# GRU recurrence started after a short early convolution, with the rest of the convolution placed between its products

## The chip, the cores and the metric

The kernel runs on one core of a Trainium2 chip. The metric is the device time of one execution in microseconds (us); lower is better.

## The reference

`x` is (128, 64, 512): batch B, steps T, channels D. `cond` (128, 512) serves twice: as the taps of a depthwise causal convolution and as the GRU's first state.

```python
y = conv_general_dilated(x, cond[:, None, :], window_strides=(1,), padding=[(127, 0)],
                         feature_group_count=512, ...) + b     # causal, one kernel per channel
x = x + y
# GRU over 64 steps, h0 = cond, on rows x[:, t]
gi = x_t @ W_ih + b_ih;  gh = h @ W_hh + b_hh                  # (128, 1536) each
r = sigmoid(i_r + h_r);  z = sigmoid(i_z + h_z);  n = tanh(i_n + r * h_n)
h = (1 - z) * n + z * h
out = x + swapaxes(hs, 0, 1)
```

The sequence axis of `x` has 64 steps, of the 128 taps the last 64 count. Of a channel, y is a 64 x 64 triangular Toeplitz matrix times the channel's (64, 128) slab of x. `x` in float32 is 16.8 MB, `W_ih` and `W_hh` 3.1 MB each. The kernel runs the recurrence over the steps of x in reverse row order of its scratch (`T - 1 - t`), because the Toeplitz matrices are built reversed.

## The kernel before, in words

**Stage one, convolution.** SP loads all of x into SBUF (`x_sb`, L328): channels in two halves c, each with steps on 64 partitions for two groups of 128 channels (`half`). Meanwhile TensorE builds the Toeplitz matrices by shifting the taps (L678), ACT and DVE copy them out (`toep_span`). Then 512 matmuls of 128x128 in full float32 (L695, `bank<-diag,x_sb`) convolve a pair of channels each; ACT spreads the Toeplitz matrices into block-diagonal `diag` (L496), DVE evicts each bank with the bias into `stage` or `kept` (L578), and SP stores these to the scratch tensor `xres` in HBM (L317, L335). The weights come behind them on SP's queue (L362), 32 partitions per DMA.

**Weights.** fp32r products carry a float32 number as two parts: ACT copies the high part (L513), DVE and POOL subtract for the low part (L297).

**Stage two, recurrence.** 64 steps, each 72 matmuls of 128x512 in fp32r (L715: for each of six gate products, four blocks of 128 channels by three products of parts): h into r, n, z; then, for the next step, x into r and n; four transposes of h (L704); x into z. The order is written out in `step`, the same on each engine: L525 for ACT, L610 for DVE, L764 for PE, L416 for SP. Between them DVE adds biases (L623, L629, L631, L640), ACT does sigmoid and tanh (L532, L534, L536), and DVE forms h and out (L642 to L655). SP stores `out_t` and loads x of four steps later, once with 256-byte runs (`xt`, L372) and once transposed by quads with 128-byte runs (`x_quads`, L380).

## Time and profile before

| what | value |
|---|---|
| device time, three runs | 1250.76, 1250.97, 1252.44 us; median 1250.97 |
| span of the profiled execution | 1249.1 us |
| PE busy | 1207.4 us (97%), x5508 |
| DVE busy, ACT busy, POOL busy | 663.6, 343.1, 16.0 us |
| DMA queue q1 (SP's) | 246848 packets, 91.45 MB, 31.9% of 16 engines |
| bytes over the span | 74 GB/s mean |

The page gives no device time of the profiled execution itself; its span lies 1.9 us under the median of the runs. PE is TensorE's matmuls, PEld its weight loads, DVE is VectorE, ACT ScalarE, POOL GpSimd, SP SyncE, which issues most DMAs. A matmul's busy time is longer than its spacing, as matmuls overlap in the pipeline: the distance between starts is what one costs in a full stream. A DMA share over 1 means that packets' recorded times overlap.

### The profile page before, as it was taken

The page shows a single profiled execution, that of the slowest core. Times are in us where ns is not written, and L with a number is a line of the kernel's source. Part 1 is how long each engine was busy: PE and PEld are TensorE (multiplying, and loading weights), DVE is VectorE, ACT ScalarE, POOL GpSimd, SP SyncE. Part 2 cuts the span into 40 slices and gives each one's busy share as a digit, 9 for nine tenths or more (in the row PEclk, how much of TensorE's full clock was granted, in tenths as well). Part 3 has the DMA queues.
Part 4 walks back from the last instruction along what each step waited for, and adds up shares of the span by engine and source line. Part 5 has one row for each costly group of instructions (what it writes and reads, how often), then busy time and mean ns, then how long its engine had stood idle before and what let it go on. Part 6 is the DMA issues. An engine that isn't in the chain of part 4 may idle for free.

```text
span 1249.1 us, 14699 instructions
## 1 busy us (share of the span) xinstructions
PE 1207.4 (97%) x5508; PEld 1019.2 (82%) x5508; DVE 663.6 (53%) x1015; ACT 343.1 (27%) x474; POOL 16.0 (1%) x20
## 2 busy tenths in 40 slices
PE   5499989999999999999999999999999999999998
PEld 5499978888888888888888888888888888888886
DVE  5255685555555455555555555555555555555554
ACT  6266661212212122212221211222121212122111
POOL 1000040000000000000000000000000000000000
PEclk9699999999999999999999999999999999999999
DMA  9996758222112222221222222122222211222200
GB/s 189 208 265 214 160 159 270 51 51 51 46 38 42 50 50 50 50 46 38 42 50 50 50 50 47 38 41 50 50 50 50 47 39 40 50 50 50 50 18 18
DMA packets 247730, 92.55 MB, mean 74 GB/s; under 512 B 203168, under 2 KB 236704, under 8 KB 246432
## 3 DMA queue, kind: packets, MB, share of 16 engines
q1 hardware_dynamic: 246848, 91.45, 31.9%
q10 hardware_dynamic: 864, 0.85, 0.3%
q8 instruction: 12, 0.20, 0.1%
q14 instruction: 6, 0.05, 0.0%
HBM read 58.72 MB, written 33.55 MB: 74 GB/s over the span
## 4 chain that ended last, share of the span: by engine, by line
PE 94%; DMA 4%; ACT 1%; POOL 0%; DVE 0%; SPq 0%; issue 0%; ACTq 0%; DVEq 0%
PE bank L715 83%; PE bank L695 9%; DMA x_sb<-in_x_dram 4%; PE bank L704 2%; ACT w_ih_hi L513 1%; ACT w_hh_hi L513 0%; POOL w_hh_lo L297 0%; DVE stage L578 0%; SPq L328 0%; DVE h_less_n L646 0%; DVE h L648 0%; DVE pre_z L640 0%; ACTq L317 0%; SPq L312 0%; ACT xT_hi L505 0%
## 5 line engine op out<-in xcount | busy, mean ns | idle before, releaser
L715 PE MATMUL bank<-w_ih_hi,xT_hi 128*128 128x512 f32 x768 | 305.5, 398 | 1.3 <-DVE w_ih_lo L297 1.1
L715 PE MATMUL bank<-w_hh_hi,hT_hi 128*128 128x512 f32 x768 | 298.9, 389 | 1.2 <-DVE w_hh_lo L297 0.8
L715 PE MATMUL bank<-w_ih_hi,xT_lo 128*128 128x512 f32 x768 | 300.0, 391 | 0.0
L715 PE MATMUL bank<-w_ih_lo,xT_hi 128*128 128x512 f32 x768 | 299.3, 390 | 0.0
L715 PE MATMUL bank<-w_hh_hi,hT_lo 128*128 128x512 f32 x768 | 298.8, 389 | 0.0
L715 PE MATMUL bank<-w_hh_lo,hT_hi 128*128 128x512 f32 x768 | 298.8, 389 | 0.0
L715 PEld LDWEIGHTS bank<-w_hh_hi,hT_hi 128*128 128x128 f32 x768 | 144.2, 188 | 31.8 <-issue 1.9
L715 PEld LDWEIGHTS bank<-w_ih_hi,xT_hi 128*128 128x128 f32 x768 | 144.3, 188 | 30.9 <-POOL w_ih_lo L297 1.0
L715 PEld LDWEIGHTS bank<-w_ih_hi,xT_lo 128*128 128x128 f32 x768 | 144.1, 188 | 31.0
L715 PEld LDWEIGHTS bank<-w_hh_hi,hT_lo 128*128 128x128 f32 x768 | 144.2, 188 | 29.9
L715 PEld LDWEIGHTS bank<-w_hh_lo,hT_hi 128*128 128x128 f32 x768 | 144.2, 188 | 29.9
L715 PEld LDWEIGHTS bank<-w_ih_lo,xT_hi 128*128 128x128 f32 x768 | 144.5, 188 | 28.2
L695 PE MATMUL bank<-diag,x_sb 128*128 128x128 f32 x512 | 112.9, 385 | 26.2 <-DMA x_sb<-in_x_dram 24.9
L564 DVE TENSOR_TENSOR hT_lo<-bank,hT_hi 128x512 fp32r<-128x512 f32 x64 | 44.3, 692 | 174.5 <-ACT hT_hi L539 174.5
L695 PEld LDWEIGHTS bank<-diag,x_sb 128*128 128x128 f32 x512 | 112.5, 313 | 26.6 <-issue 26.6
L539 ACT ACTIVATE hT_hi<-bank 128x512 fp32r<-128x512 f32 x63 | 37.7, 598 | 283.3 <-PE bank L704 283.3
L631 DVE TENSOR_TENSOR new_h<-bank,bias_hh 128x512 f32<-128x512 f32 x64 | 44.2, 691 | 127.8 <-PE bank L715 127.8
L534 ACT ACTIVATE n_gate<-pre_n 128x512 f32<-128x512 f32 x64 | 40.4, 632 | 224.6 <-DVE pre_n L636 224.6
L496 ACT ACTIVATE diag<-toep_span 64x512 f32<-64x512 f32 x64 | 74.7, 1168 | 59.5 <-PE bank L695 58.7
L629 DVE TENSOR_TENSOR pre_r<-bank,bias_rz 128x512 f32<-128x512 f32 x64 | 44.2, 691 | 78.9 <-PE bank L715 78.9
L532 ACT ACTIVATE r<-pre_r 128x512 f32<-128x512 f32 x64 | 40.4, 632 | 155.3 <-DVE pre_r L629 155.3
L623 DVE TENSOR_TENSOR new_x<-bank,bias_ih 128x512 f32<-128x512 f32 x64 | 44.3, 692 | 54.2 <-PE bank L715 52.5
(54 smaller groups left out, 796.6 us busy)
## 6 DMA issues: line engine op xcount, KB each, us to landing
xt<-xres SPq DMA_DIRECT2D x128, 128.0 KB, 2.6
out_dram<-out_t SPq DMA_DIRECT2D x64, 256.0 KB, 2.1
x_quads<-xres SPq DMA_DIRECT2D x252, 64.0 KB, 2.4
x_sb<-in_x_dram SPq DMA_DIRECT2D x2, 4096.0 KB, 35.3
...
```

The source lines that it names most:

```text
L496: m = nc.scalar.activation(diag[p % 2][rows, :].rearrange("s (i h u) -> s i h u", i=PIECE, h=2)[:, :, half, :], toep[c][rows, i0 * T:(i0 + ...
L513: nc.scalar.activation(hi[which][:, cols], raw[which][:, cols], ACT.Copy).then_inc(w_hi_ready, 1)
L532: nc.scalar.activation(r[:, :], pre_r[:, :], ACT.Sigmoid).then_inc(r_ready, 1)
L534: nc.scalar.activation(n_gate[:, :], pre_n[:, :], ACT.Tanh).then_inc(n_ready, 1)
L539: nc.scalar.activation(hT_hi[:, :], ps_hT[:, :], ACT.Copy).then_inc(hT_hi_ready, 1)
L564: nc.vector.tensor_tensor(lo_out[:, :], full[:, :], hi_in[:, :].bitcast(F32), ALU.subtract).then_inc(lo_ready, 1)
L623: nc.vector.tensor_tensor(new_x[:, :], ps_in[:, :], bias_ih[:, N:NG], ALU.add).then_inc(new_x_ready, 1)
L629: nc.vector.tensor_tensor(pre_r[:, :], ps_r[:, :], bias_rz[:, R:R + D], ALU.add).then_inc(pre_r_ready, 1)
L631: nc.vector.tensor_tensor(new_h[:, :], ps_hn[:, :], bias_hh[:, N:NG], ALU.add).then_inc(new_h_ready, 1)
L695: mm = nc.tensor.matmul(bank[m % 8][:, j % BPAIRS * P:(j % BPAIRS + 1) * P], x_sb[c][:, :].rearrange("s (b i) -> s i b", b=B)[:, i0 + j, : ...
L704: mm = nc.tensor.transpose(psum[:, k * P:(k + 1) * P], block_of(k), ident[:, 0:P])
L715: mm = nc.tensor.matmul(psum[:, :], a[:, rows], w[which][:, cols], start=start and n == 0, stop=stop and n == 2)
```

## The change

The convolution is split in time. Names new in it:

- **Early part.** The steps 0 to 15 (`EARLY`) of all channels are convolved first, in float32: `x_early` holds 8 groups of 64 channels on 16 partitions each (eight DMAs, 4.2 MB, 256-byte runs), `toep_early` is laid out from `kernel_full` in HBM by 16 DMAs on ACT's queue (64-byte runs). 64 matmuls of 128x128 (L698), DVE evicts them into `early_result`, 16 banks, two ahead of each block of weights it splits (L590). SP stores the result in four quarters of eight DMAs (L292), each from 16 partitions (4.2 MB in all), behind all weight loads.
- **Step 0** takes its x row from `x_row` directly. On ACT it waits for x of step 1 (`xT_loaded`), whose load SP issues after all quarters are stored, and for `early_stored`, before its first sigmoid.
- **Bulk part.** The 48 other steps of all channels (as a 64 x 64 product) are convolved in 128 banks of two pairs of channels: four matmuls of 128x256 in fp32r each (L730). Up to ten banks go between the 24 blocks of products of each of the steps 1 to 13 (`bulk_bank`, `POINTS`). x comes a second time, in 8 units of 64 channels with 128-byte runs into 64 partitions (2.1 MB each, two buffers); the Toeplitz matrices come from `kernel_parts` in HBM by overlapping rows (64 blocks, 262 KB each, 256-byte runs, four buffers). ACT copies the high part of x (`split`), DVE subtracts the low part; a bank is evicted half by ACT (`first_half`, two operations of 128 columns), half by DVE (`second_half`). The result is stored in 16 stages of two DMAs from 48 partitions (786 KB the two).
- **Recurrence.** Same 72 matmuls and four transposes per step. Biases are written into PSUM by ACT ahead of the products (`put_bias`, four per step), so that DVE's four bias additions go; `x_quads` and its transpose go; x is loaded transposed, 512-byte runs (`load_xT`); out is formed transposed and turned by DVE (L657, L664), stored by four DMAs.

```diff
-SLICE = 32
-PIECE = 8
+EARLY = 16
+POINTS = 10
+BULK_FIRST, BULK_LAST = 1, 13
...
-            load_x(0, 0, B)
-            load_x(1, 0, 3 * QUARTER)
+            for c in range(C0):
+                sp.dma_start(
+                    x_early[c * EARLY:(c + 1) * EARLY, :].rearrange("s (b g) -> s b g", g=G0),
+                    x[:, 0:EARLY, c * G0:(c + 1) * G0].rearrange("b s g -> s b g"),
+                ).then_inc(x_early_loaded, 16)
+            for n in range(QUARTERS):
+                sp.wait_ge(early_evicted, (n + 1) * NB0 // QUARTERS)
+                per = G0 // QUARTERS
+                for c in range(C0):
+                    e = place_of(c * G0 + n * per)
+                    sp.dma_start(xres[LATE:T, e:e + per, :].rearrange("u g b -> u (g b)"),
+                                 quarter[n][c * EARLY:(c + 1) * EARLY, :]).then_inc(early_stored[n], 16)
...
+            def load_xT(u, back):
+                sp.dma_start(
+                    xT[u][:, :].rearrange("p (k b) -> p k b", b=B),
+                    xres[bass.ds(back, 1), :, :].rearrange("o (k p) b -> p (o k) b", p=P),
+                ).then_inc(xT_loaded[u], 16)
...
+                    ch = unit * 2 * UNIT + c * UNIT
+                    bs = slice(b4 * B // 4, (b4 + 1) * B // 4)
+                    sp.dma_start(
+                        x_unit[unit % 2][c * T:(c + 1) * T, :].rearrange("s (b g) -> s b g", g=UNIT)[:, bs],
+                        x[bs, :, ch:ch + UNIT].rearrange("b s g -> s b g"),
+                    ).then_inc(x_unit_loaded[unit % 2], 16)
...
+                    source = bass.AP(first.tensor, first.offset, [[1, T], [P, 2 * BLOCK], [1, T]])
+                    sp.dma_start(
+                        toep[j % T_RING][c * T:(c + 1) * T].bitcast(F32).rearrange(
+                            "s (n e) -> s n e", e=P)[:, :, c * T:(c + 1) * T],
+                        source,
+                    ).then_inc(toep_loaded[j % T_RING], 16)
...
+                    e = place_of(unit * 2 * UNIT + c * UNIT + g)
+                    sp.dma_start(xres[0:LATE, e:e + STAGE, :].rearrange("u g b -> u (g b)"),
+                                 stage[n % 2][c * T:c * T + LATE, :]).then_inc(stage_stored[n % 2], 16)
...
+            for n in range(QUARTERS):
+                sp.wait_ge(early_stored[n], 16 * C0)
+            load_xT(1, T - 2)
+            sp.wait_ge(early_done, NB0)
+            sp.wait_ge(k_parts_stored, 16 * QUADS)
+            for b4 in range(4):
+                load_x_quarter(0, b4)
+            for j in range(T_RING):
+                load_toep(j)
+            load_xT(2, T - 3)
+            load_xT(3, T - 4)
+            for b4 in range(4):
...
+                if m % 2 == 0 and m >= 2 and m // 2 + 3 < NBLOCK:
+                    sp.wait_ge(conv_done, m)
+                    load_toep(m // 2 + 3)
+                if m % 8 == 2 and m > 2:
+                    store_stage(m // 8 - 1)
+                unit, b4 = (m + 21) // 16, (m + 21) % 16 // 2
+                if m % 2 and 2 <= unit < NUNIT and b4 < 4:
+                    if b4 == 0:
+                        sp.wait_ge(x_lo_ready, (unit - 1) * UNIT // BLOCK)
+                    load_x_quarter(unit, b4)
...
-                    rows = slice(half * T, (half + 1) * T)
-                    m = nc.scalar.activation(
-                        diag[p % 2][rows, :].rearrange("s (i h u) -> s i h u", i=PIECE, h=2)[:, :, half, :],
-                        toep[c][rows, i0 * T:(i0 + PIECE) * T].rearrange("s (u i) -> s i u", u=T), ACT.Copy)
+                for c in range(C0):
+                    first = kernel_full[c * G0 + half * G0 // 2:(c + 1) * G0, T - EARLY:T]
+                    act.dma_start(
+                        toep_early[half][c * EARLY:(c + 1) * EARLY, :].rearrange(
+                            "s (g e) -> s g e", e=P)[:, :, c * EARLY:(c + 1) * EARLY],
+                        bass.AP(first.tensor, first.offset, [[1, EARLY], [P, G0 // 2], [1, EARLY]]),
+                    ).then_inc(toep_early_loaded[half], 16)
...
+            def put_bias(psum, bias, done):
+                nc.scalar.activation(psum[:, :], bias, ACT.Copy).then_inc(done, 1)
...
+                if j >= HL_RING:
+                    act.wait_ge(conv_done, 2 * (j - HL_RING) + 2)
+                unit = j // (UNIT // BLOCK)
+                act.wait_ge(x_unit_loaded[unit % 2], 16 * 8 * (unit // 2 + 1))
+                nc.scalar.activation(part_block(j, 0), x_block(j), ACT.Copy).then_inc(x_hi_ready, 1)
...
+                    nc.scalar.activation(tmp[m % 2][:, pair * B:(pair + 1) * B],
+                                         conv_bank[m % 3][:, pair * 2 * B:pair * 2 * B + B], ACT.Identity,
+                                         bias=bias_pair[:, 2 * m + pair:2 * m + pair + 1]).then_inc(tmp_ready, 1)
...
+                first_half(bulk_bank(t - 1, POINTS - 1))
+                if not last(i, u):
+                    act.wait_ge(xT_loaded[(u + 1) % RING], 16 * (i + 1))
+                    act.wait_ge(gi_done, t + 1)
+                    nc.scalar.activation(xT_hi[:, :], xT[(u + 1) % RING][:, :], ACT.Copy).then_inc(xT_hi_ready, 1)
+                split(split_block(t, 0))
+                first_half(bulk_bank(t, 0))
+                if not isinstance(i, bass.RuntimeValue) and t == 0:
+                    for n in range(QUARTERS):
+                        act.wait_ge(early_stored[n], 16 * C0)
+                act.wait_ge(gh_r_done, t + 1)
+                nc.scalar.activation(r[:, :], ps_r[:, :], ACT.Sigmoid).then_inc(r_ready, 1)
...
+                if not isinstance(i, bass.RuntimeValue) and t == BULK_FIRST - 1:
+                    split(0)
+                    split(1)
...
-                nc.vector.tensor_tensor(
-                    stage(g).rearrange("b (u h i) -> b i h u", h=2, i=SLICE)[:, i0:i0 + BPAIRS],
+                if g == R:
+                    for _ in range(2):
+                        early_evict(evicted)
+                        evicted += 1
+                if not on_pool(w, k, g):
+                    dve.wait_ge(w_hi_ready, n + 1)
+                    low_weights(nc.vector, w, k, g).then_inc(w_lo_ready, 1)
...
+                nc.vector.tensor_tensor(
+                    stage[s % 2][:, at:at + 2 * B].rearrange("p (g b) -> p g b", b=B),
+                    conv_bank[m % 3][:, :].rearrange("p (g l b) -> p g l b", l=2, b=B)[:, :, 1, :],
+                    tmp[m % 2][:, :].rearrange("p (g b) -> p g b", b=B),
+                    ALU.add).then_inc(stage_ready, 1)
...
-                for j in range(PIECE):
-                    m = (p * PIECE + j) // BPAIRS
-                    mm = nc.tensor.matmul(
-                        bank[m % 8][:, j % BPAIRS * P:(j % BPAIRS + 1) * P],
-                        x_sb[c][:, :].rearrange("s (b i) -> s i b", b=B)[:, i0 + j, :],
-                        diag[p % 2][:, j * P:(j + 1) * P], start=True, stop=True)
+                if slot == 0 and n >= 3:
+                    pe.wait_ge(early_evicted, n - 2)
+                mm = nc.tensor.matmul(conv_bank[n % 3][:, slot:slot + B], toep_early[half][:, g_half * P:(g_half + 1) * P],
+                                      x_early[:, :].rearrange("p (b g) -> p g b", g=G0)[:, g, :],
+                                      start=True, stop=True)
...
+                if m >= 3:
+                    pe.wait_ge(stage_ready, m - 2)
+                elif m == 0:
+                    pe.wait_ge(early_evicted, NB0)
+                if m % 2 == 0:
+                    j = m // 2
+                    pe.wait_ge(toep_loaded[j % T_RING], 32 * (j // T_RING + 1))
+                    pe.wait_ge(x_lo_ready, j + 1)
+                for pair in range(2):
+                    j, slot = (2 * m + pair) // BLOCK, (2 * m + pair) % BLOCK
+                    for low in range(2):
+                        at = (slot * 2 + low) * P
+                        mm = nc.tensor.matmul(conv_bank[m % 3][:, pair * 2 * B:(pair + 1) * 2 * B],
+                                              toep[j % T_RING][:, at:at + P],
+                                              parts[j % HL_RING][:, slot * 2 * B:(slot + 1) * 2 * B],
+                                              start=low == 0, stop=low == 1)
+                mm.then_inc(conv_done, 1)
...
+                        g = group[0]
+                        group[0] += 1
+                        if g * POINTS // GROUPS != (g + 1) * POINTS // GROUPS:
+                            bulk(bulk_bank(t, g * POINTS // GROUPS))
...
+                pe.wait_ge(hT_lo_ready, t + 1)
+                product(ps_r, hT_hi, hT_lo, 1, R, True, gh_r_done)
+                pe.wait_ge(bias_hn_put, t + 1)
+                product(ps_hn, hT_hi, hT_lo, 1, N, True, gh_n_done)
+                product(ps_z, hT_hi, hT_lo, 1, Z, True, gh_z_done)
```

SP's queue at the start. Before, from the first DMA to the weights:

```order
L312 DMA taps_sb<-in_cond_dram 64x2x128
L328 DMA x_sb_49<-in_x_dram 64x128x128 x2
L328 DMA x_sb_50<-in_x_dram 64x96x128 x2
L317 DMA xres<-stage_60 128x2048 [waits stage_ready]
...
L335 DMA xres<-stage_64 128x4096 [waits stage_ready]
L362 DMA w_ih_raw<-in_L_cond_W_ih_dram 32x1536 [waits xres_stored2,diag_ready]
```

The same place in the change, up to the loads of the bulk part:

```order
L271 DMA h<-in_cond_dram 128x4x32 x4
L271 DMA x_row<-in_x_dram 128x4x32 x4
L277 DMA x_early<-in_x_dram 16x128x64 x8
L285 DMA w_ih_raw<-in_L_cond_W_ih_dram 32x1536 x16
L285 DMA w_hh_raw<-in_L_cond_W_hh_dram 32x1536 x16
L292 DMA xres<-early_result_93 16x2048 [waits early_evicted]
...
L296 DMA xT_75<-xres 128x4x128 [waits early_stored2,early_stored3,early_stored1,early_stored0]
L305 DMA x_unit_55<-in_x_dram 64x32x32 [waits k_parts_stored,early_done]
L305 DMA x_unit_55<-in_x_dram 64x32x32 x7
L316 DMA toep_ring<-kernel_parts 64x8x64 x8
```

The weights moved ahead of every store; the stores, 128 partitions wide before, are 16 wide, and x of step 1 is loaded only behind them.

ACT in step 0 of the change (`r` is the first gate):

```order
L513 ACTIVATE xT_hi_79<-xT1_75 128x512 [waits gi_done,xT_loaded1]
L520 ACT_TABLE_LOAD [waits early_stored3,early_stored2,gh_r_done,early_stored1]
L520 ACTIVATE r_66<-bank0 128x512 [waits early_stored0]
L469 ACTIVATE bank0<-bias_rz_81 128x512 [waits r_ready]
L528 ACTIVATE n_gate_68<-q_69 128x512 [waits pre_n_ready]
```

Before, ACT had no wait for a store there; now the first sigmoid stands behind the load of x of step 1 and behind all quarters.

PE in step 1 of the change, from its first product of h:

```order
L708 MATMUL bank<-w_hh_hi,hT_hi 128x512 [waits hT_lo_ready]
L708 MATMUL bank<-w_hh_lo,hT_hi 128x512
L708 MATMUL bank<-w_hh_hi,hT_lo 128x512
...
L730 MATMUL bank<-x_parts_58,toep_ring 128x256 [waits x_lo_ready,toep_loaded0,early_evicted]
L730 MATMUL bank<-x_parts_58,toep_ring 128x256 x3
L708 MATMUL bank<-w_hh_hi,hT_hi 128x512
```

A bank of the convolution (four matmuls) stands after the third block of products, and so on at ten places of the step; the products behind it on PE wait with it.

## Rows read from the trace of the kernel before

**Rows 1.** The page: span, and the chain that ended last, by engine

```profile
span 1249.1 us, 14699 instructions
...
PE 94%; DMA 4%; ACT 1%; POOL 0%; DVE 0%; SPq 0%; issue 0%; ACTq 0%; DVEq 0%
```

**Rows 2.** The chain in order of time: start us, us, what (x count)

```profile
2.42 44.97 DMA x_sb<-in_x_dram
47.64 56.41 PE bank L695 x256
...
105.34 56.46 PE bank L695 x256
...
189.74 0.44 PE bank L704 x4
190.18 16.37 PE bank L715 x72
206.99 16.38 PE bank L715 x72
...
1232.00 10.93 PE bank L715 x48
1242.95 0.70 DVE pre_z L640
```

**Rows 3.** Timeline of PE near 10 us, 256-column fp32r matmuls: start us, us, instruction

```profile
10.11 0.28 PE L678 MATMUL bank<-taps_lo,window 128*128 128x256 f32 x1
10.22 0.28 PE L678 MATMUL bank<-taps_hi,window 128*128 128x256 f32 x1
```

**Rows 4.** Windows: stretch, us, busy of PE PEld DVE ACT POOL, PEclk, DMA share, GB/s

```profile
9.00:20.00 11.00, 11.00 (x94) 11.00 (x94) 10.78 (x24) 10.72 (x23) 0.00 (x0) 1.00 1.23 205
78.00:82.00 4.00, 4.00 (x20) 4.00 (x19) 2.56 (x3) 2.67 (x3) 0.00 (x0) 1.00 1.01 426
122.00:132.00 10.00, 10.00 (x48) 10.00 (x47) 5.72 (x7) 6.50 (x7) 0.00 (x0) 1.00 1.02 219
132.00:136.00 4.00, 4.00 (x20) 4.00 (x19) 2.58 (x3) 2.83 (x3) 0.00 (x0) 1.00 1.11 244
175.00:177.00 2.00, 1.74 (x8) 1.48 (x9) 2.00 (x5) 1.60 (x4) 0.84 (x1) 1.00 1.05 292
259.00:260.00 1.00, 1.00 (x7) 0.81 (x5) 0.38 (x1) 0.00 (x0) 0.00 (x0) 1.00 0.99 157
```

**Rows 5.** DMA issues: queue op xcount, KB each, us to landing

```profile
out_dram<-out_t SPq DMA_DIRECT2D x64, 256.0 KB, 2.1
xt<-xres SPq DMA_DIRECT2D x128, 128.0 KB, 2.6
```

**Rows 6.** Timeline of SP near 257 us: start us, us, instruction xcount

```profile
257.31 2.05 SPq L380 DMA_DIRECT2D x_quads<-xres  x4
```

**Rows 7.** Windows, TensorE idle and started again: columns as in Rows 4

```profile
26.00:28.00 2.00, 0.00 (x0) 0.00 (x0) 0.00 (x0) 1.86 (x2) 0.00 (x0) 0.55 1.24 215
51.00:53.00 2.00, 2.00 (x12) 2.00 (x10) 1.05 (x1) 1.51 (x2) 0.00 (x0) 0.50 1.22 205
53.00:55.00 2.00, 2.00 (x11) 2.00 (x11) 1.15 (x2) 0.95 (x2) 0.00 (x0) 0.88 1.22 205
```

**Rows 8.** Groups by line and shape: busy us, mean ns, idle before

```profile
L496 ACT ACTIVATE diag<-toep_span 64x512 f32<-64x512 f32 x64 | 74.7, 1168 | 59.5 <-PE bank L695 58.7 <-DVE toep_span L558 0.4
L646 DVE TENSOR_TENSOR h_less_n<-z,h_less_n 128x512 f32<-128x512 f32 x64 | 44.4, 693 | 10.7 <-ACT z L536 10.6
L532 ACT ACTIVATE r<-pre_r 128x512 f32<-128x512 f32 x64 | 40.4, 632 | 155.3 <-DVE pre_r L629 155.3
L539 ACT ACTIVATE hT_hi<-bank 128x512 fp32r<-128x512 f32 x63 | 37.7, 598 | 283.3 <-PE bank L704 283.3
L578 DVE TENSOR_TENSOR stage<-bank,conv_bias 128x512 f32<-128x512 f32 x32 | 32.1, 1033 | 55.9 <-PE bank L695 55.9
L530 ACT ACT_TABLE_LOAD x15 | 19.2, 1283 | 22.9 <-DVE xT L618 22.9
L505 ACT ACTIVATE xT_hi<-bank 128x256 fp32r<-128x256 f32 x2 | 0.7, 373 | 4.9 <-PE bank L737 4.9
```

924 lines of the change are left out of this document (431 added, 493 removed).

## Prediction

> **What bounds the kernel now.** I read the page first: the chain that ended last is TensorE for 94% and DMA for 4% of the 1249.1 us span [rows 1]. The chain in order of time then splits the span in two [rows 2]. Until 162 us it is the convolution: 45.0 us of waiting for the first half of x, then twice 56.4 us of matmuls. From 189.74 us on it is the recurrence: 72 matmuls in 16.37 us (0.2273 us each) and four transposes in 0.44 us, 16.80 us a step, to the last products at 1242.93 us; 6.2 us of gates and store follow. The reader should see that a step has no idle time on PE, and that before the first full step 190 us pass. The change can only win in those 190 us, and it pays for it inside the steps. From the windows I then read what DMAs reach by shape, since the change replaces wide transfers by narrow ones.
>
> **What goes.** Waiting for half of x, both convolution stretches and the wait for the last weights, all before 189.74 us. DVE's bias additions and the transpose of x lie beside a busy PE: nothing gained.
>
> **Rates of the DMAs.** Into 64 partitions x comes at 205 GB/s; from 128 partitions the stores leave at 426, or 3.3 GB/s for each partition; into 32 partitions at a time the weights come at 219 to 244, say 230, or 7.2 per partition; bias rows into 128 partitions (with others) at 292; 128-byte runs into 32 partitions at 157 [rows 4]. So 64 partitions get half of what 128 get, and 32 as much as 64. For 16 partitions the trace has no row. Upper end: 230, if again nothing is lost. Lower end: 51, the 3.2 per partition of the 64. I take 16 x 7 = 110, since 7 per partition is about the highest that any row shows, and the 32-partition row is the nearest. The Trainium skill ("SBUF — State Buffer", Door 1: The DMA port swizzle) says that bandwidth goes by how many of 16 ports the partitions reach, eight for both 32 and 64, and lists 104 GB/s for partitions 0 to 15; this trace agrees for 64 against 128 and has nothing on 16. By that page's 104 the two terms of 38 us below would be 40 us each. For 256-byte runs into 64 partitions the ends are 157 and 205; I take 180, the middle.
>
> **The start, to the moment E at which the early result is stored.** SP's queue is served in order.
> - Eight loads of h and x_row, each issued in 0.51 us (2.05 for four [rows 6]), from 0.8 us: 4.9 us.
> - x_early, 4.19 MB at 110 GB/s: 38 us, to 43.
> - ACT's queue shares the engines: 8192 runs of 64 bytes at no more than the 0.82 ns that a 128-byte run takes (128 B at 157 GB/s): 6.7 us, and 2.3 MB of other data at 292: 7.9. I take 12 of these 14.6, as a little falls before x_early starts (ends 0 and 14.6). To 55.
> - Weights, 6.29 MB at 230: 27.3 us. To 82.3.
> - The quarters, 4.19 MB at 110: 38.1, and 2.1 to land [rows 5]. E = 122.5.
>
> Beside this: 64 early matmuls at 0.22 us, or 0.44 at half clock (256 in 56.41 at mostly full clock, rows 2), are 14 to 28 us from 55 on; weights are split as they come; the products of step 0 end by about 100. That is hidden under the stores; without that cover it would be the bound at 95 to 100.
>
> **Step 0 after E.** Load of x for step 1: 0.5 + 2.6 [rows 5]; high part 0.63, table load 1.28, r 0.63, bias into PSUM 0.6 [rows 8]: E + 6.3. Then 24 products 5.5, transposes 0.4, 12 products 2.7. PE has stood still for over 20 us; in the trace it fell to half clock (0.55, then 0.50) when idle and needed about 6 us of matmuls to come back [rows 7], here 3 us of loss. Step 0 ends at E + 18.
>
> **Steps 1 to 15.** 15 x 16.80 = 252.0. The bulk adds 512 matmuls of 256 columns; such a stream has starts 0.117 us apart [rows 3]: 59.7. Together 312.
>
> Do the other engines keep up? A full bulk step lasts 16.80 + 40 x 0.117 = 21.5 us. ACT: nine operations of 512 at 0.6, twenty of 128 columns at 0.26 (from 0.598 for 512 and 0.373 for 256 [rows 8]), five splits that read with a stride; L496, with a stride, takes 1.17, against 0.63 without. Sum 5.5 + 5.2 + 5.9 = 16.6. DVE: nine at 0.69, ten at 0.42, five at 1.03 (as L578): 15.6. Both fit. The tightest place is hT_hi, which stands behind three splits and four evictions: about 7.7 us of ACT from gh_z on, against 7.3 of PE, then 1.4 to the low part of h, covered by 12 products and two banks (3.7 us). About 1.5 us is left.
>
> DMA hardly fits. Per 16 banks, 34.3 us of PE: one unit of x 2.1 MB at 157, 13.4; eight Toeplitz blocks 2.1 MB at 180, 11.7; two stages 1.57 MB from 48 partitions, at 205 as for 64: 7.7 (ends 3.7 at 426 and 14 at 110); out and transposed x of 1.6 steps, 3.7. That is 36.4, 2 over, eight times: 17 us, less what the prefetch of four blocks absorbs. I take 10 (ends 0 and 50). Bulk also starts with a backlog: unit 0, four blocks and x of two steps stand in the queue before unit 1, so that x of step 2 arrives at about E + 24, and ACT's r of step 1 behind it: 5 us. Named after the wait: PE at the bulk matmul stands for `toep_loaded` or `stage_ready`, and the products of the gates wait behind it. Step 15 ends at E + 18 + 312 + 15 = E + 345.
>
> A second rule of the skill ("DMA: Bandwidth & Descriptors", How a descriptor splits into AXI transactions) charges a run that starts off a 256-byte boundary for bytes that it fetches and drops. The Toeplitz rows start 4 bytes apart, so nearly all are such runs. No row of this trace has one. By that page a run would take 15 instead of 11 beats on average, and a block a third longer, which would be worth an estimated 25 us more; it is in neither sum.
>
> **Steps 16 to 63.** 47 x 16.80 = 789.8, 36 products 8.2. Then z 0.63, two DVE operations 1.4, transposes 0.6, two DVE operations 1.4, four DMA issues 1.5, landing 2.1: 7.6, against 6.2 now.
>
> **Sum.** 122.5 + 345 + 789.8 + 8.2 + 7.6 = 1273 of span, against 1249.1. The median of the runs lies 1.9 us over the profiled span: 1275 us, slower by 24 us (1.9%). Before gave 189.74 us to the start; now step 0's transposes come at E + 15, or 137; 52 us are won there, and 60 of bulk matmuls, 15 of waits and 1.4 at the end are paid.
>
> **Rivals.**
> - *Faster: 16 partitions cost nothing more than 32.* x_early at 230 takes 18, the quarters 18 at 230, or 10 at 426: 40 to 48 us less, 1227 to 1235; with stage stores at 426 too the waits of 10 go: 1217. Price 1225. The decision falls at about 160 GB/s for both. For it: 32 partitions get what 64 get. Against it: 64 do not get what 128 get, so something other than the 16 engines counts. Chance 0.25.
> - *Far slower: narrow runs cost by their number.* x_sb's 512-byte runs took 2.5 ns each at 205 GB/s (512/205). If a 128-byte run of x cost half of that, 1.25 ns instead of 0.82, the bulk's 131,072 runs would take 164 us instead of 107, and DMA would bound the bulk: about 45 us more, 1320. For it: these runs come from the same tensor x as those slow ones; the row at 157 GB/s reads `xres`. Against: that row. Chance 0.10.
> - *ACT or DVE bounds the bulk.* If a split costs 1.8 us on ACT (its stride is 128 bytes, L496 read 32), ACT's 19.8 of 21.5 with waits in between puts hT_hi late by about 1 us in 13 steps: 1288. Chance 0.05, inside the range.
> - *The bulk does not fall between the products.* PE executes in order and the listed order has it there; no chance.
>
> **Numbers.** The forecast case has 0.60 and reaches by itself from 1244 (no DMA waits, ACT's queue hidden, consecutive narrow DMAs overlapping a little) to 1310 (stages at 110 GB/s). The faster rival lies at 1214 to 1243. The range of 1214 to 1310 leaves out the far slower rival and little more of the tails. About 0.2% is what a measurement here can tell from no change, 1248.5 to 1253.5: the forecast's low end puts 0.05 there, and 0.01 under it. Faster 0.26, same 0.05, slower 0.69.
>
> **What would show it.** Right: DMA at about 110 GB/s while `x_early` loads and while `early_result` is stored; the first sigmoid of step 0 at about 127 us, preceded by an idle PE at half clock; steps 14 and later at 16.80 us; steps 1 to 13 at 21.5 to 24 us with waits at L730 for `toep_ring`. Wrong: over 200 GB/s in the two narrow stretches and E near 80; or bulk steps at exactly 21.5 us, which would say that DMA fits with ease; or bulk steps over 26 us; or waits at L730 for ACT's and DVE's evictions.

## The result and the profile after

The changed kernel takes 1268.35 us (median of 4 runs, 1265.81 to 1273.29) beside 1251.57 (4 runs, 1250.76 to 1252.44): a ratio of 1.0138, 95% interval 1.0114 to 1.0162, slower by 1.4%. The forecast was 1275 and slower. The ratios here and below are those of all runs of a kernel to runs of the kernel before, taken beside them. The profiled span is 1265.0 us, forecast at 1273.

The page of the changed kernel, to be held against [rows 1]: the span, and the chain that ended last, by engine and by line.

```profile
span 1265.0 us, 14934 instructions
...
PE 86%; DMA 3%; ACTq 3%; DVE 2%; ACT 2%; SPq 2%; issue 1%; POOL 0%; DVEq 0%
PE bank L708 78%; PE bank L730 4%; DMA bias_hn<-in_L_cond_b_hh_dram 2%; PE bank L675 2%; ACTq L442 2%; SPq L305 1%; DVE w_ih_lo L255 1%; PE bank L698 1%; ACT tmp L503 1%; DMA kernel_full<-k_full 1%; ACT x_parts L493 1%; ACT bank L469 1%; SPq L316 0%; DVE early_result L581 0%; DMA xT<-xres 0%
```

The second entry of the lower row, after the products and the bulk, is a transfer that the prediction never costed: the load of `bias_hn`, 256 KB. The chain in order of time (start us, us, what) shows its place at the start, as [rows 2] did for the kernel before.

```profile
48.11 28.93 DMA bias_hn<-in_L_cond_b_hh_dram
77.04 0.07 issue
77.11 2.35 POOL bias_rz L402
79.46 0.02 issue
79.48 2.15 ACT bank L469 x4
81.64 0.56 ACT w_ih_hi L484
...
82.22 1.29 DVE w_ih_lo L255 x2
83.51 1.20 DVE early_result L581 x2
...
96.88 9.13 PE bank L698 x40
106.02 0.02 issue
106.04 0.70 DVE early_result L581
...
110.67 2.84 DMA xres<-early_result
```

Read it downwards: the last bias lands at 77.04, GpSimd adds two of them, ScalarE copies four into the banks, and only then splits the first weights (L484), 24 splits in a row. VectorE takes the low parts and, between them, the evictions of the early convolution, which free the banks for the early matmuls. The last eviction starts at 106.04, the last store lands at 113.5. The prediction had E, the same moment, at 122.5, by another road.

Windows of the changed kernel (columns as in Rows 4): x_early loading, the weights, and two moments while the quarters are stored (the first of them one microsecond long).

```profile
20.00:30.00 10.00, 0.00 (x0) 0.00 (x0) 0.00 (x0) 0.00 (x0) 0.00 (x0) 0.50 1.44 109
...
50.00:60.00 10.00, 7.54 (x34) 7.33 (x35) 2.67 (x4) 1.31 (x3) 0.00 (x0) 0.68 1.09 249
...
96.00:97.00 1.00, 0.14 (x2) 0.12 (x1) 1.00 (x3) 0.00 (x0) 0.00 (x0) 0.50 0.79 262
109.00:111.00 2.00, 2.00 (x10) 1.65 (x10) 0.00 (x0) 0.00 (x0) 0.00 (x0) 1.00 0.91 221
```

The load into 16 partitions ran at 109 GB/s; 110 was taken. The stores from 16 partitions ran at 221 to 262 in these two windows, though 110 was taken for them too.

The steps are read from the starts of hT_hi on ScalarE (timeline: start us, us, instruction, idle before and its releaser): here the end of step 0, step 1, and step 11, the longest.

```profile
128.27 0.60 ACT L547 ACTIVATE hT_hi<-bank 128x512 fp32r<-128x512 f32 x1 [4.14 <-PE bank L675]
152.76 0.64 ACT L547 ACTIVATE hT_hi<-bank 128x512 fp32r<-128x512 f32 x1
...
354.11 0.60 ACT L547 ACTIVATE hT_hi<-bank 128x512 fp32r<-128x512 f32 x1
380.43 0.60 ACT L547 ACTIVATE hT_hi<-bank 128x512 fp32r<-128x512 f32 x1
```

Steps 1 to 13 take 24.49, 22.99, 23.64, 21.77, 21.77, 23.18, 21.75, 21.91, 21.95, 22.39, 26.32, 21.78 and 20.74 us, together 294.7; from step 14 on a step is 16.80, as before. A step with ten banks and no wait is 21.77, so a bank costs 0.497 us. 13 x 16.80 + 128 x 0.497 is 282.0, and 12.7 us are waits. What a wait costs is seen in step 11 (windows, columns as in Rows 4):

```profile
365.00:370.00 5.00, 5.00 (x30) 4.33 (x29) 3.17 (x6) 3.85 (x8) 0.00 (x0) 1.00 0.81 206
370.00:375.00 5.00, 1.98 (x9) 1.45 (x8) 3.04 (x5) 2.52 (x6) 0.00 (x0) 0.88 0.74 179
375.00:380.00 5.00, 5.00 (x24) 4.28 (x23) 0.42 (x1) 1.72 (x4) 0.00 (x0) 0.78 0.94 242
```

PE stands still for 3 us in the second window, and its granted clock is 0.88 there and 0.78 in the next, where it is busy throughout and issues 24 matmuls instead of 30. A wait of 3.0 us so lengthened the step by 4.55.

What it waited for is seen on SyncE's queue (timeline of SyncE, then of PE):

```profile
363.61 1.84 SPq L327 DMA_DIRECT2D xres<-stage  x2
365.51 4.38 SPq L361 DMA_DIRECT2D out_dram<-outZ  x4
...
370.42 5.33 SPq L316 DMA_DIRECT2D toep_ring<-kernel_parts  x8
...
374.31 1.19 PE L730 MATMUL bank<-x_parts,toep_ring 128*128 128x256 f32 x4 [3.02 <-issue]
```

The next Toeplitz block is issued at 370.42, behind the store of the step's output, and landed at 374.22, 0.09 us before the matmul that needs it. The stops of PE of over 1 us at L730 in steps 2, 3 and 6 end in the same way, each 0.09 us after its block has landed. In step 1 it is another load: ScalarE stood 4.8 us for x of step 2 (`xT`), and the gates with it.

### The profile page after: what moved, and what is told of

Same layout as the page of the kernel before. It is cut to its first block, busy times and chain, and to the rows that moved or that the text cites. A ratio compares the mean times of both kernels' runs of the same rounds, so it can differ in the third digit from the quotient of the medians.

```text
span 1265.0 us, 14934 instructions
## 1 busy us (share of the span) xinstructions
PE 1180.7 (93%) x5520; PEld 982.5 (78%) x5520; DVE 536.7 (42%) x803; ACT 491.9 (39%) x928; POOL 18.9 (1%) x18
## 4 chain that ended last, share of the span: by engine, by line
PE 86%; DMA 3%; ACTq 3%; DVE 2%; ACT 2%; SPq 2%; issue 1%; POOL 0%; DVEq 0%
PE bank L708 78%; PE bank L730 4%; DMA bias_hn<-in_L_cond_b_hh_dram 2%; PE bank L675 2%; ACTq L442 2%; SPq L305 1%; DVE w_ih_lo L255 1%; PE bank L698 1%; ACT tmp L503 1%; DMA kernel_full<-k_full 1%; ACT x_parts L493 1%; ACT bank L469 1%; SPq L316 0%; DVE early_result L581 0%; DMA xT<-xres 0%
## 5 line engine op out<-in xcount | busy, mean ns | idle before, releaser
L708 PEld LDWEIGHTS bank<-w_ih_lo,xT_hi 128*128 128x128 f32 x768 | 144.9, 189 | 26.5
L631 DVE TENSOR_TENSOR q<-bank,r 128x512 f32<-128x512 f32 x64 | 44.1, 689 | 205.4 <-PE bank L708 205.4
L528 ACT ACTIVATE n_gate<-q 128x512 f32<-128x512 f32 x64 | 40.5, 633 | 173.8 <-DVE q L633 173.8
L730 PEld LDWEIGHTS bank<-x_parts,toep_ring 128*128 128x128 f32 x512 | 77.8, 190 | 22.6 <-DVE stage L613 8.0
L503 ACT ACTIVATE tmp<-bank,bias_pair 128x128 f32<-128x128 f32 x256 | 78.3, 365 | 41.0 <-PE bank L730 41.0
L513 ACT ACTIVATE xT_hi<-xT 128x512 fp32r<-128x512 f32 x63 | 39.8, 632 | 135.1 <-PE bank L708 108.3
L730 PE MATMUL bank<-x_parts,toep_ring 128*128 128x256 f32 x512 | 82.7, 284 | 8.8 <-DVE stage L613 5.5
L469 ACT ACTIVATE bank<-bias_rz 128x512 f32<-128x512 f32 x128 | 77.1, 603 | 32.2 <-POOL bias_rz L402 28.1
L602 DVE TENSOR_TENSOR x_parts<-x_unit,x_parts 128x512 fp32r<-128x512 f32 x64 | 70.6, 1104 | 38.1 <-ACT x_parts L493 38.0
## 6 DMA issues: line engine op xcount, KB each, us to landing
w_ih_raw<-in_L_cond_W_ih_dram SPq DMA_DIRECT2D x16, 192.0 KB, 13.5
```

Of the source, the lines that this page charges most:

```text
L469: nc.scalar.activation(psum[:, :], bias, ACT.Copy).then_inc(done, 1)
L503: nc.scalar.activation(tmp[m % 2][:, pair * B:(pair + 1) * B], conv_bank[m % 3][:, pair * 2 * B:pair * 2 * B + B], ACT.Identity, bias=bias ...
L513: nc.scalar.activation(xT_hi[:, :], xT[(u + 1) % RING][:, :], ACT.Copy).then_inc(xT_hi_ready, 1)
L528: nc.scalar.activation(n_gate[:, :], q[:, :], ACT.Tanh).then_inc(n_ready, 1)
L602: nc.vector.tensor_tensor(part_block(j, 1), x_block(j), part_block(j, 0).bitcast(F32), ALU.subtract).then_inc(x_lo_ready, 1)
L631: nc.vector.tensor_tensor(q[:, :], ps_hn[:, :], r[:, :], ALU.mult).then_inc(reset_h_ready, 1)
```

## Experiments

In the diffs a line of "..." marks what is left out. Steps are timed by hT_hi, as above. xT(n) is x of step n, transposed.

### The biases first

The four loads of the GRU's biases go from the end of ScalarE's queue to its head.

```diff
+            act.dma_start(bias_rz[:, :], b_ih[0:N].partition_broadcast(P)).then_inc(bias_loaded, 16)
+            act.dma_start(bias_tmp[:, :], b_hh[0:N].partition_broadcast(P)).then_inc(bias_loaded, 16)
+            act.dma_start(bias_in[:, :], b_ih[N:NG].partition_broadcast(P)).then_inc(bias_loaded, 16)
+            act.dma_start(bias_hn[:, :], b_hh[N:NG].partition_broadcast(P)).then_inc(bias_loaded, 16)
             def tap_columns(tile):
...
-            act.dma_start(bias_rz[:, :], b_ih[0:N].partition_broadcast(P)).then_inc(bias_loaded, 16)
...
```

> The four loads of the GRU's biases (1.5 MB) are issued first on ACT's queue instead of last; nothing else changes. Theory A (the start is gated by these biases: the last landed at 77.1 us, POOL's sum and ACT's four bias writes stood behind it and the split of the weights, and with it DVE's evictions of the early result, stood behind ACT): the split of w_ih begins when its first block has landed, 55 to 60 us instead of 81.6, DVE's last eviction comes at about 85 to 95 instead of 106, and the transposes of step 0 at 112 to 118 instead of 127.8; total 1250 to 1256 us. Rival B (the start is bound by the bytes of the DMA queues whatever their order, x_early, weights and stores in series): the early result is stored at most 4 us earlier and the total is 1262 us or more.

Measured: 1255.74 us (1253.31 to 1258.91, 5 runs), ratio to before 1.0038 (1.0025 to 1.0052). The chain of this kernel in order of time:

```profile
54.82 28.43 PE bank L698 x128
83.27 0.70 DVE early_result L581
...
91.00 2.90 DMA xres<-early_result
```

All 64 early matmuls (two records to each, 0.444 us together) now run in one piece. The last eviction is 22.8 us earlier, and step 0 ends at 106.49 instead of 128.27. That is 21.8 us won, but the span fell by 13.5 only: steps 1 to 13 took 303.0 instead of 294.7, with 27.0, 25.5, 25.7 and 26.9 in steps 1, 2, 6 and 11. The total lies in the range of theory A, but step 0 ended earlier than it said (112 to 118).

### The same transfers, ScalarE's order changed

The wait for the biases and the four copies of them stand behind the splits of w_ih instead of ahead of them.

```diff
-            act.wait_ge(bias_rz_ready, 1)
-            act.wait_ge(banks_opened, 1)
-            put_bias(ps_r, bias_rz[:, R:R + D], bias_r_put)
...
                 if (w, k, g) == (1, 0, R):
                     act.wait_ge(k_parts_stored, 16 * QUADS)
+                    act.wait_ge(bias_rz_ready, 1)
+                    act.wait_ge(banks_opened, 1)
+                    put_bias(ps_r, bias_rz[:, R:R + D], bias_r_put)
...
```

> The changed kernel with its transfers as they are: only ScalarE's order is changed. The wait for the four GRU biases and the four copies of them into the banks stand behind the twelve splits of w_ih and ahead of those of w_hh, not ahead of all 24. Theory A, the start is held by the splits that stand behind that wait on ScalarE's in-order queue (the biases land at 77.0, the splits start at 81.6 though w_ih is there from about 58): the w_ih splits start near 58, half of the 16 evictions follow them, and those behind w_hh's splits end near 95 instead of 106; transposes of step 0 at 117, total 1258 to 1263 with some us given back in steps 1 and 2. Theory B, what helped when the biases were loaded first was another thing (their transfers out of the way of the weights): 1267 to 1270.

Measured: 1257.17 us (1256.15 to 1259.08, 5 runs), ratio 1.0045 (1.0032 to 1.0058); just under the 1258 that was expected at best. ScalarE's timeline in this kernel:

```profile
54.11 1.67 ACT L483 ACTIVATE w_ih_hi<-w_ih_raw 128x512 fp32r<-128x512 f32 x3 [2.81 <-DMA w_ih_raw<-in_L_cond_W_ih_dram]
...
69.85 1.67 ACT L483 ACTIVATE w_ih_hi<-w_ih_raw 128x512 fp32r<-128x512 f32 x3 [3.49 <-DMA w_ih_raw<-in_L_cond_W_ih_dram]
79.32 1.12 ACT L469 ACTIVATE bank<-bias_rz 128x512 f32<-128x512 f32 x2 [7.80 <-issue]
```

The biases are put into the banks at 79.32, as late as before, and the w_ih splits go ahead of them, each triple as its weights land. Step 0 ends at 115.84, 12.4 us earlier. So 12.4 of the 21.8 us that the biases first won at the start come from the order on ScalarE alone, with every transfer where it was: the work queued behind the wait for the biases cost them. The other 9.4 are not parted here. The w_hh splits still stood behind the biases, to 81.4, and the transfers themselves are moved only in the run with the biases first.

### What the bulk costs, and what its transfers cost

First the late convolution is left out altogether.

```diff
-            if isinstance(t, int) and BULK_FIRST <= t <= BULK_LAST:
-                m = (t - BULK_FIRST) * POINTS + point
-                return m if m < NBANK else None
             return None
...
-                            load_xT(late % RING, T - 1 - late)
+                            load_xT(late % RING, LATE)
```

> The late convolution is left out altogether: its x, its Toeplitz loads, its matmuls, evictions and stores; the steps from 16 on take one row of the early result. Theory: steps 1 to 13 take 16.8 us as the others, so the difference to the change is the full price of the bulk, 59.7 to 63 us of matmuls and 15 of waits: total 1190 to 1194 us. If the bulk cost less than 70 us, the waits are not its own and lie in the start; then the total is over 1198.

Measured: 1190.2 us (1188.39 to 1190.73, 4 runs), 78 under the changed kernel; all steps from 1 on are 16.80, but step 1 with 17.26. Step 0 ends at 127.27, so the start owes the bulk 1 us at most.

In the next kernel each Toeplitz load from the fifth block on brings an eighth of its bytes.

```diff
-                    source = bass.AP(first.tensor, first.offset, [[1, T], [P, 2 * BLOCK], [1, T]])
+                    width = 2 * BLOCK if j < T_RING else 1
+                    source = bass.AP(first.tensor, first.offset, [[1, T], [P, width], [1, T]])
...
-                            "s (n e) -> s n e", e=P)[:, :, c * T:(c + 1) * T],
+                            "s (n e) -> s n e", e=P)[:, 0:width, c * T:(c + 1) * T],
```

> From the fifth Toeplitz block on each block's DMA brings one of its eight parts (an eighth of the bytes), so the late convolution is computed with other matrices; matmuls, waits and the order stay. Theory A (DMA just fails to keep up in steps 1 to 13, as in the sum's term of 10 us): steps 3, 6 and 11, which took 23.6, 23.2 and 26.3 us, come to 21.8, and the whole is 8 to 14 us faster, 1255 to 1260. Rival B (the waits in these steps come from the order of ACT and DVE, whose evictions stand behind the gates): no step changes by more than 0.3 us and the total stays within 2 us of 1268.

Measured: 1259.8 us (1257.41 to 1260.07, 4 runs), 8.5 less. By the profile the span is 7.1 us shorter. Of the 8.8 us of waits in steps 3 to 13, 7.3 are gone, and the 1.5 left lie in step 11. Step 0 ended 2.9 us earlier, which the edit doesn't explain, but steps 1 and 2 took 3.0 longer (25.9 and 24.7 us): step 2 ends at 175.9 here and at 175.8 in the changed kernel. What the span lost it lost in steps 3 to 13, where the thinned loads are.

The same was then done to the biases-first kernel, and to its x units as well:

```diff
-                    bs = slice(b4 * B // 4, (b4 + 1) * B // 4)
+                    bs = slice(b4 * B // 4, b4 * B // 4 + (B // 4 if unit < 2 else B // 32))
```

> The kernel with the biases first (1255.7 us), whose Toeplitz blocks from the fifth on and whose x units from the third on bring one eighth of their bytes, so the late convolution uses old data and its output is not the reference's; every matmul, eviction, store and issue is still there. Its steps 1 to 13 took 303.0 us against 283.0 for 13 times 16.80 and 128 banks. Theory A, transfers set what is above 283: steps 3 to 13 take 21.77 us each, what is left is at most the start's 9 us in steps 1 and 2, total 1237 to 1245, under the kernel before. Theory B, the waits are of ScalarE and VectorE (splits, tmp, stage beside the gates): they stay, 1250 or more.

Measured: 1239.27 us (1238.73 to 1240.58, 4 runs), ratio 0.9901 (0.9887 to 0.9916). Step 1 is 27.11 and every step from 2 to 12 is 21.73 to 21.78. Windows of this kernel, then of the changed kernel:

```profile
150.00:250.00 100.00, 100.00 (x536) 86.01 (x535) 70.11 (x112) 74.02 (x158) 0.00 (x0) 1.00 0.36 85
250.00:400.00 150.00, 150.00 (x796) 128.83 (x796) 100.31 (x161) 105.45 (x228) 0.00 (x0) 1.00 0.33 79
```

```profile
150.00:250.00 100.00, 96.93 (x517) 82.89 (x518) 68.55 (x110) 72.03 (x154) 0.00 (x0) 1.00 0.86 181
250.00:400.00 150.00, 145.54 (x762) 123.54 (x761) 98.55 (x157) 105.26 (x225) 0.00 (x0) 0.99 0.83 180
```

ScalarE and VectorE are about as busy in both; the DMA share falls, from 0.86 to 0.36, and PE never stands in these stretches. The waits of steps 2 to 13 are the transfers' and no engine's. Thin loads are both moved and issued faster, so this run does not tell the rate from the order of issue.

### Two edits of the order of issue that did not help

First the loads of the x units 2 to 7 are spread over 16 banks instead of 8.

```diff
-                unit, b4 = (m + 21) // 16, (m + 21) % 16 // 2
-                if m % 2 and 2 <= unit < NUNIT and b4 < 4:
+                unit, b4 = (m + 21) // 16, (m + 21) % 16 // 4
+                if (m + 21) % 4 == 0 and 2 <= unit < NUNIT:
```

> Only the times at which SyncE issues the x_unit loads of units 2 to 7 are changed: a pair of loads at every fourth bank instead of at every second, so that they are spread over 16 banks and not bunched in 8. Bytes and instructions are the same. In the changed kernel steps 1 to 13 take 294.7 us, 12.7 more than 13 times 16.80 and 128 banks of 0.497; 8.8 of these lie in steps 3 to 11, the most in step 11 (4.6). Theory A, the bunched loads hold SyncE's queue and make the Toeplitz blocks late: steps 6 and 11 lose their waits, 1262 us (1260 to 1265). Theory B, it is the mean load of the DMA queues: no change, 1267 to 1270, and waits of the same sum in other steps.

Measured: 1267.46 us (1265.92 to 1269.88, 4 runs), theory B by the total. In the profiled execution (1269.88, the slowest of the four) steps 1 to 13 take 298.5 us against 294.7, and where step 6 had its wait, step 7 now has one (26.7).

Then, in the changed kernel, the load of xT(2) goes ahead of the first x unit.

```diff
             load_xT(1, T - 2)
...
+            load_xT(2, T - 3)
             for b4 in range(4):
                 load_x_quarter(0, b4)
             for j in range(T_RING):
                 load_toep(j)
-            load_xT(2, T - 3)
```

> Only one transfer is moved: SyncE issues the load of xT(2) right after xT(1), ahead of the first x unit and the first four pairs of Toeplitz loads. Theory A, step 1 is long (24.49 us against 21.77 for a step with ten banks and no wait) because xT_hi waited 4.8 us for that load: step 1 becomes 21.8 to 22.5 and the total 1266. Theory B, it waits as long for the first Toeplitz blocks or for the x unit, which all come half a microsecond later: no change, 1268 to 1269.

Measured: 1277.77 us (1270.89 to 1278.48, 5 runs), 9.4 slower by the medians, some 6 by the ratios, 1.0187 (1.0164 to 1.0210) beside 1.0138 (1.0114 to 1.0162); neither theory had that. Step 1 did fall, to 22.42. But SyncE's queue was still issuing the second unit until 148.9 and the Toeplitz blocks of the next banks only from 152.5, and step 2, which now began sooner, waited longer: 29.25 us. In the changed kernel these two moments were 146.6 and 149.8. The windows of this kernel:

```profile
150.00:156.00 6.00, 1.64 (x9) 1.02 (x7) 1.99 (x3) 1.98 (x4) 0.00 (x0) 0.87 0.79 174
156.00:162.00 6.00, 5.09 (x18) 4.40 (x19) 1.73 (x3) 1.14 (x4) 0.00 (x0) 0.56 0.63 141
```

PE is busy for 1.64 us of the first 6 and gets 18 matmuls through in the next, at a clock of 0.56. Steps 6 and 11 waited longer as well (26.5 and 29.4); why these did is open.

### SyncE's order on top of the earlier start

A first try put three edits on the biases-first kernel at once: the first x unit on ScalarE's queue, xT(2) ahead of the Toeplitz blocks, and the spread units (not shown again).

```diff
+            act.wait_ge(early_done, NB0)
+            for b4 in range(4):
+                for c in range(2):
+                    bs = slice(b4 * B // 4, (b4 + 1) * B // 4)
+                    act.dma_start(
+                        x_unit[0][c * T:(c + 1) * T, :].rearrange("s (b g) -> s b g", g=UNIT)[:, bs],
+                        x[bs, :, c * UNIT:(c + 1) * UNIT].rearrange("b s g -> s b g"),
+                    ).then_inc(x_unit_loaded[0], 16)
...
             load_xT(1, T - 2)
...
-            for b4 in range(4):
-                load_x_quarter(0, b4)
+            load_xT(2, T - 3)
```

> The changed kernel with four edits: the four GRU biases first on ScalarE's queue (as in the run with the biases first, 1255.7 us), the first x unit issued from ScalarE's queue as soon as the early matmuls are done instead of from SyncE's after the early stores, xT(2) right after xT(1), and the x_unit loads of units 2 to 7 spread over 16 banks. Theory A, what that run gave back (steps 1 and 2 of 27.0 and 25.5 us, 9.0 above 21.77 each) was SyncE's queue at the start, 12.7 us for the first unit's issues ahead of the Toeplitz blocks and xT(2), and the waits of steps 6 and 11 (9.1) were the bunched loads: transposes of step 0 at 106, steps 1 and 2 below 23, steps 6 and 11 near 22, together 1242 us (1239 to 1246), faster than the kernel before. Theory B, the loads themselves and not the order of their issue set these waits (the DMA rate of 150 to 200 GB/s in that stretch is the limit): 1252 to 1256.

Measured: 1255.95 us (1252.6 to 1258.93, 11 runs), nothing won over the biases first. ScalarE's timeline in it:

```profile
91.68 17.54 ACTq L488 DMA_DIRECT2D x_unit<-in_x_dram  x6
109.32 0.63 ACT L520 ACTIVATE xT_hi<-xT 128x512 fp32r<-128x512 f32 x1 [25.18 <-issue]
```

The issues, done beside SyncE's, hold ScalarE until 109.3, while the loads of xT(1) and xT(2) had been issued by 96.6; step 0 ends 15 us later than with the biases first. Steps 1 to 6, however, are 21.75 to 21.88 now, and steps 7 and 11 wait (26.4 and 26.2). That the loads were there in time because the recurrence began later is a reading; with three edits at once the run does not show it.

Then one edit at a time, again on the biases-first kernel. Half of the second unit is issued inside step 1:

```diff
-            for b4 in range(4):
+            for b4 in range(2):
                 load_x_quarter(1, b4)
...
+                if m in (3, 5):
+                    load_x_quarter(1, 2 + m // 5)
```

> The kernel with the biases first (1255.7 us), where only the last four of the eight loads of the second x unit are moved from ahead of the output of step 0 to behind the third and fifth bank of step 1. Theory A, in steps 1 and 2 SyncE's order of issue binds (12.5 us of these issues stood ahead of the Toeplitz blocks of step 1, which were issued at 130.8 and landed at 134): step 1 falls from 27.0 to about 23 and the total to 1250 to 1253. Theory B, the rate binds and the wait comes back later, in step 2 or 3, and with it the lower clock that follows an idle TensorE: 1254 to 1258.

Measured: 1250.67 us (1245.85 to 1257.38, 12 runs), 5 less, ratio 0.9998 (0.9984 to 1.0012). The total is what theory A said, but not the step: in the profiled execution, the fastest of the twelve (1245.85), step 1 is 26.3 and it is step 2 that falls, from 25.5 to 21.6; step 6 falls from 25.7 to 22.8, and step 11 stays (27.0).

Then the store of a step's output, which held SyncE's queue until outZ was there, moves behind the first two banks of the next step (`tail` holds that wait, the store and the loads of xT):

```diff
+                if isinstance(t, int) and t <= BULK_LAST:
+                    for point in range(POINTS):
+                        bulk(t, point)
+                        if point == 1 and t >= 1:
+                            tail((t - 1) // RING, (t - 1) % RING)
```

> The kernel of the run before (biases first, half of the second x unit later; 1250.7 us) with one more edit: in steps 1 to 13 SyncE stores the output of a step, and loads the xT that takes its place, behind the first two banks of the next step and not at the step's end. So its queue is not held by the wait for outZ while Toeplitz blocks could be issued. Theory A, the wait that is left in step 11 (5.2 us above 21.77) and those of 1 us in steps 3 and 6 are Toeplitz blocks that stand behind that wait and the four stores (6.6 us in step 10): step 11 below 23.5, total 1245 (1243 to 1248). Theory B, the transfers' rate sets them, whatever the order: the same sum of waits in other steps, 1249 to 1252.

Measured: **1243.07 us** (1241.09 to 1245.45, 5 runs), ratio to before **0.9938** (0.9925 to 0.9951): faster than both kernels, with nothing left out. Step 11 falls from 27.0 to 21.8, as theory A had it; but steps 5 and 7, which did not wait, now do (23.6 and 24.6), and step 1 waits most (27.2). In the two profiles steps 1 to 13 take 292.5 us and 293.4, so most of the 4.8 us between them lie at the end of step 0 (104.7 and 108.6), which this edit doesn't touch. That the kernel is faster is shown by the ratios, 0.9938 after 0.9998; how much of it is this one edit's is not. Against the biases-first kernel steps 1 to 13 are 10.5 us shorter, which is the two edits together.

Two more edits on top: the load of xT(2) goes ahead of the first x unit, and two of that unit's eight loads go to ScalarE's queue.

```diff
-            for b4 in range(4):
+            load_xT(2, T - 3)
+            for b4 in range(1, 4):
                 load_x_quarter(0, b4)
...
+            act.wait_ge(early_done, NB0)
+            for c in range(2):
+                act.dma_start(
+                    x_unit[0][c * T:(c + 1) * T, :].rearrange("s (b g) -> s b g", g=UNIT)[:, 0:B // 4],
+                    x[0:B // 4, :, c * UNIT:(c + 1) * UNIT].rearrange("b s g -> s b g"),
+                ).then_inc(x_unit_loaded[0], 16)
```

> The kernel of the run above with two more edits at the start: xT(2) is loaded right after xT(1), and the first two of the eight loads of the first x unit are issued on ScalarE's queue as soon as the early matmuls are done (all of them there took 25.7 us and held xT_hi of step 0 by 12). Theory A: ScalarE is free again by 95, before xT(1) lands; SyncE's first x unit takes 9.4 us and not 12.5; step 1 falls from 26.3 to about 22.5 and the total is 3 to 4 us below that of the run above, 1241 (1239 to 1245). Theory B: the shared transfers delay the early stores and xT(1) by as much as they gain: the same total as the run above, within 1.5 us.

Measured: 1243.03 us (1240.48 to 1247.85, 6 runs), the same. Two issues on ScalarE took 7.3 us (timeline of this kernel):

```profile
82.61 7.32 ACTq L500 DMA_DIRECT2D x_unit<-in_x_dram  x2
97.51 0.63 ACT L532 ACTIVATE xT_hi<-xT 128x512 fp32r<-128x512 f32 x1 [14.30 <-DMA xT<-xres]
```

Step 1 is 21.88, as theory A had it, and 5.3 us are won there. But xT_hi comes 2.3 us later than in the run above (95.22 there), and steps 7 and 11 wait 2 us more together. The total is theory B's; it lies in theory A's range too.

### The rates by themselves

A program with nothing but transfers of the shapes in dispute, one stage after the other:

> Only transfers, one shape after another, each stage waiting for the one before. Theory A (a DMA's rate goes by how many partitions it touches at once, half for 64 and 32, a quarter for 16): 256-byte runs of x into 16 partitions 105 GB/s, into the same 16 again the same, into 32 and 64 about 180 to 205, into 128 over 250; stores from 16 partitions 110 GB/s both when the DMAs go round the partitions and when all use the same 16; from 48 partitions 160; from 128 over 400. Rival B (in the change's trace stores of 16 partitions ran at 221 GB/s between 109 and 111 us, so DMAs on different partitions overlap): round the partitions 200 or more, on the same 16 about 110. 128-byte runs of x into 64 partitions: 157 by the row of before, 100 if they cost half of what x_sb's 512-byte runs cost. Toeplitz blocks with shifted rows: 180, or a third less than with aligned rows if a shifted start costs.

Its windows, each inside one stage, in order: x into 16 partitions in rotation, into the same 16 each time, into 32, into 64, into 128; stores of 128 KB from 16 partitions in rotation, always from the same 16, stores from 48, from 128; runs of 128 bytes; Toeplitz blocks as in the kernel, and with rows that all start on the same boundary (columns: stretch, us, busy of DVE and POOL, PEclk, DMA share, GB/s).

```profile
85.00:110.00 25.00, 0.00 (x0) 0.00 (x0) 1.00 1.33 118
122.00:132.00 10.00, 0.00 (x0) 0.00 (x0) 1.00 1.33 109
143.00:161.00 18.00, 0.00 (x0) 0.00 (x0) 1.00 1.31 210
166.00:182.00 16.00, 0.00 (x0) 0.00 (x0) 1.00 1.31 207
188.00:202.00 14.00, 0.00 (x0) 0.00 (x0) 1.00 1.15 262
206.00:224.00 18.00, 0.00 (x0) 0.00 (x0) 1.00 0.89 226
230.00:265.00 35.00, 0.00 (x0) 0.00 (x0) 1.00 0.98 102
275.00:290.00 15.00, 0.00 (x0) 0.00 (x0) 1.00 0.92 270
296.00:302.00 6.00, 0.00 (x0) 0.00 (x0) 1.00 1.01 425
306.00:318.00 12.00, 0.00 (x0) 0.00 (x0) 1.00 0.98 153
322.00:332.00 10.00, 0.00 (x0) 0.00 (x0) 1.00 0.84 187
335.00:345.00 10.00, 0.00 (x0) 0.00 (x0) 1.00 0.85 193
```

So 110 GB/s is right for one group of 16 partitions, loaded or stored. It is wrong for stores that follow each other from different groups: 226. That number is no ceiling of the transfers, since SyncE took 18.0 us to issue the 32 stores, 0.56 us for 128 KB, which is an estimated 233 GB/s. The Toeplitz loads were issued 0.68 us apart, an estimated 193 GB/s, so the issuing seems to set these two rows as well; by the DMA share of 0.84 and 0.85 a shifted row took the DMA engines an estimated 2% more time per byte, if anything. (In the last stage all 64 rows were read from one place, so it is not a pure test of the shift.) The biases-first kernel shows more, where the evicted quarters wait in SyncE's queue for nothing but their turn:

```profile
84.00:90.00 6.00, 6.00 (x28) 4.98 (x27) 1.16 (x2) 0.72 (x2) 1.51 (x1) 1.00 1.04 413
```

That is nearly the rate of stores from all 128 partitions, 426 [rows 4]. The loads into rotating groups gained little, 118 against 109; whether that is their direction or their size of 512 KB was not tried.

## Why the prediction was right, and where it was not

**The total.** The span was forecast at 1273 and is 1265.0. Up to the transposes of step 0, which start 0.7 us ahead of hT_hi, it had 137 and got 127.6; from there to the end 1136 and 1137.4. The loss has the forecast's shape, a start won and bulk paid in the steps. The start, though, came out within 10 us only because two larger errors of opposite sign met, and that was luck.

**x_early and ScalarE's queue: right.** 100 to 116 GB/s for 110; the first early matmul at 52.5 for "to 55". The Trainium skill's table figure of 104 ("SBUF — State Buffer", Door 1: The DMA port swizzle) would have done as well: 109 was measured. The step that led to 110 was weaker than its result: "64 partitions get half of what 128 get" set a load beside a store, and by loads alone it is 207 for 64 and 262 for 128.

**The quarters, 38.1 us: the step that failed first.** It took the rate of one group of 16 partitions for a stream that visits eight. In the trace the stores run at 221 to 262 GB/s in the windows shown, and at 413 in the biases-first kernel. Of the faster rival's condition, both transfers at over 160, half came true: the quarters, but not x_early. "E near 80" did not follow, because E had come to hang on another chain.

**"That is hidden under the stores": the step that failed second, in the other direction.** The early matmuls, the splits and step 0's products were to end by 95 to 100. They ended at 122.4, and the first sigmoid came at 118.3, not 127, with no idle PE ahead of it: the sum looked at each of these by its own duration and by when its data lands, not by what stands ahead of it in its queue. The 24 splits stood behind a wait for four biases, these behind 38 other issues of ScalarE's queue, and the last of them, 256 KB, took 28.9 us to land beside SyncE's loads. VectorE's evictions stood between the low parts of those weights. Freed, the same chain ends at 99.6 (the last w_hh product of the biases-first kernel): the forecast of 95 to 100 was that of a kernel without this wait. Between the two, by ScalarE's order alone, 12.4 us come back. Within it "14 to 28 us" for the early matmuls was low, since 0.22 us is one of the two records of such a product: at full clock they take 28.4. (The convolution before has 512 records at L695 as well, of 256 matmuls.)

**Clock at the start: not lost.** 3 us were set for a PE that comes back from 20 idle us. It had no such pause, since the products of step 0 ran up to its gates.

**Bulk, 59.7 us: 4 short.** A 256-column matmul within the products costs 0.124 us and not the 0.117 of a stream of its own, so 63.6. Without the bulk the kernel is 78 us faster, against 59.7 + 15 in the sum. **DMA waits, 5 + 10: 3.9 in steps 1 and 2, and 8.8 in steps 3 to 13.** The named waits came: x of step 2 at E + 23 for "E + 24", and Toeplitz blocks late at L730. Moving that x ahead took step 1 from 24.5 to 22.4, and thin Toeplitz loads took away 7.3 of the 8.8. Steps 1 and 11, with 24.5 and 26.3 us, lay outside the "21.5 to 24". What the sum had wrong is the reason: it let the bytes fall 2 us short in every 34, but the DMA share was 0.83 to 0.86 and steps 4, 5 and 7 had no wait at all. The long wait is a block issued late, behind the store of the output; with that store moved, step 11 is 21.8 us, though 4.6 us of waits appear in steps 5 and 7. How much of the waits order alone could take away stays open. A part of each wait is the clock that falls after the stop. The rates assumed, 157 for runs of 128 bytes and 180 for Toeplitz blocks, came out at 153 and 187, and 48 partitions stored at 270 where 205 was taken. The Trainium skill ("DMA: Bandwidth & Descriptors", How a descriptor splits into AXI transactions) would have made a shifted run cost an estimated third more than an aligned one; the program of transfers shows 187 GB/s against 193, 3%, at a rate that the issuing held down. (The 25 us in the text were low even by that rule: a third of eight times 11.7 us is 31.)

**ACT and DVE: right.** Every step without a DMA wait is 21.77 us, so neither bounds. **Steps from 14 on: right**, 16.80 us. **The end: 7.9 for 7.6.**

**The rivals.** The 1320 of the narrow runs fell with 153 GB/s, near the 157 taken. The 1225 was not reached by any run: the biases first and SyncE's order give 1243, and the biases first with transfers thinned in the bulk 1239. But 1243 is under the kernel before, so what kept the change from paying was an order of issues and not its idea.
